# Attention's minus maximum as a row of the zero-padded contraction, in a two-layer sequence net on one core

## What is computed

```python
q = (x @ wq).reshape(Bq, Tq, N_KV, N_REP, HEAD_DIM)
k_lat = (x @ wk_down).reshape(Bq, Tq, N_KV, D_LAT)
v_lat = (x @ wv_down).reshape(Bq, Tq, N_KV, D_LAT)
k = jnp.einsum('bkhl,ld->bkhd', k_lat, wk_up)
scores = jnp.einsum('bqhrd,bkhd->bhrqk', q, k) * scale
scores = jnp.where(causal, scores, jnp.finfo(scores.dtype).min)
probs = jax.nn.softmax(scores, axis=-1)
```

## Time and profile before

| | |
|---|---|
| median of 3 runs | 1990.47 us (1987.96 to 1991.94) |
| the profiled execution, its own time | 1983.65 us |
| its span in the trace | 1981.8 us |
| PE busy | 1660.5 us, 84% |
| DVE busy | 1547.1 us, 78% |
| ACT busy | 1120.8 us, 57% |
| POOL busy | 754.8 us, 38% |

### The profile page before, as it was taken

The page is one execution under the profiler, slowest core; times in us unless marked ns, Lnnn a source line. Parts: engine busy times, 40 slices in busy tenths (PEclk is TensorE's granted clock), DMA queues, the critical chain, the costliest instruction groups (busy, mean ns, idle before and its releaser), DMA issues.

```text
span 1981.8 us, 26962 instructions
## 1 busy us (share of the span) xinstructions
PE 1660.5 (84%) x8352; PEld 768.2 (39%) x8352; DVE 1547.1 (78%) x2173; ACT 1120.8 (57%) x1555; POOL 754.8 (38%) x601
## 2 busy tenths in 40 slices
PE   2434487889997999889997899889998999989988
PEld 0210123344443445344443345344443445434545
DVE  1999899869995899769995899869996999641404
ACT  2445387358744786458744786458744785433232
POOL 0345555324533355324533355324533445310102
PEclk8655699899999999899999999999999999989999
DMA  7999999657955687657955787657955686500000
GB/s 197 228 221 225 227 230 210 150 135 181 230 133 141 158 216 178 156 123 183 231 131 140 159 214 181 156 126 181 232 132 141 165 209 184 130 0 0 6 1 6
DMA packets 107915, 309.48 MB, mean 156 GB/s; under 512 B 15970, under 2 KB 32244, under 8 KB 107764
## 3 DMA queue, kind: packets, MB, share of 16 engines
q1 hardware_dynamic: 93556, 279.32, 59.5%
q10 hardware_dynamic: 14208, 28.32, 4.4%
HBM read 287.67 MB, written 19.92 MB: 155 GB/s over the span
## 4 chain that ended last, share of the span: by engine, by line
PE 36%; DVE 21%; ACT 21%; issue 12%; DMA 5%; ACTq 2%; DVEq 1%; SPq 1%; POOL 0%; POOLq 0%
PE ps_pair L698 8%; PE ps_pair L795 7%; DVE sb_hst L1263 7%; ACT L919 6%; PE ps_pair L854 5%; DMA sb_ring<-spread_dram 5%; PE ps_pair L783 4%; PE ps_pair L874 3%; PE ps_pair L651 3%; ACT sb_ring L950 3%; ACT sb_mix L1099 3%; DVE sb_dd L1241 2%; DVE ps_in L1255 2%; DVE sb_nmax L1404 2%; PE ps_pair L798 2%
## 5 line engine op out<-in xcount | busy, mean ns | idle before, releaser
L1532 POOL TENSOR_TENSOR sb_hc<-sb_hst,sb_crep 128x512 f32<-128x512 f32 x512 | 659.3, 1294 | 990.0 <-DVE sb_hst L1263 617.1
L1263 DVE TENSOR_TENSOR_SCAN sb_hst<-sb_ring,ps_in 128x512 f32<-128x512 f32 x512 | 620.5, 1212 | 21.2 <-ACT sb_ring L950 13.2
L950 ACT ACTIVATE sb_ring<-sb_ring,sb_A 128x512 f32<-128x512 f32 x512 | 345.2, 713 | 227.0 <-DMA sb_ring<-spread_dram 99.5
L1255 DVE TENSOR_TENSOR ps_in<-sb_ring,ps_brow 128x512 f32<-128x512 f32 x512 | 354.3, 692 | 22.1 <-DMA sb_ring<-spread_dram 4.7
L854 PE MATMUL ps_pair<-sb_mix,sb_ew 128*128 128x512 f32 x512 | 251.3, 625 | 19.8 <-ACT sb_h L1065 9.4
L919 ACT ACT_TABLE_LOAD x193 | 247.6, 1283 | 7.3 <-DVE sb_xd L1314 3.2
L633 PE MATMUL ps_y<-sb_hc,sb_const 128*32 128x512 f32 x1024 | 154.2, 677 | 83.0 <-POOL sb_hc L1532 59.4
L795 PE MATMUL ps_pair<-sb_g,sb_h 128*128 128x512 f32 x320 | 170.5, 658 | 23.4 <-DVE sb_dd L1243 11.1
L783 PE MATMUL ps_pair<-sb_h,sb_g 128*128 128x512 f32 (+3 forms) x512 | 165.4, 452 | 6.5 <-DVE sb_nmax L1404 3.2
L854 PEld LDWEIGHTS ps_pair<-sb_mix,sb_ew 128*128 128x128 f32 x512 | 96.0, 198 | 156.7 <-issue 87.1
L874 PEld LDWEIGHTS ps_pair<-sb_ew,sb_eh 128*128 128x128 f32 x1024 | 120.6, 192 | 37.3 <-issue 13.6
(11 more groups left out here) (219 smaller groups left out, 2037.9 us busy)
## 6 DMA issues: line engine op xcount, KB each, us to landing
sb_ring<-spread_dram SPq DMA_DIRECT2D x512, 512.0 KB, 5.6
spread_dram<-sb_dd ACTq DMA_DIRECT2D x32, 512.0 KB, 3.0
sb_brep<-cut_dram ACTq DMA_DIRECT2D x16, 256.0 KB, 3.8
sb_crep<-cut_dram ACTq DMA_DIRECT2D x16, 256.0 KB, 4.2
sb_xtok<-in_L_attn_x_dram SPq DMA_DIRECT2D x8, 256.0 KB, 5.1
sb_ew<-in_L_ffn_w_dram SPq DMA_DIRECT2D x2, 1024.0 KB, 8.5
out_dram<-sb_yy ACTq DMA_DIRECT2D x8, 256.0 KB, 2.3
sb_h<-in_L_ffn_h_w_dram SPq DMA_DIRECT2D x1, 1024.0 KB, 7.0
```

The costliest lines, as they stand in the source:

```text
L950: act.activation(ring[:, n % RING, 0, :], ring[:, n % RING, 0, :], ACT.Exp, scale=A[d][:, g:g + 1]).then_inc(sem["dA"], 1)
L1255: dve.tensor_tensor(ps_in[n % 2][:], ring[:, n % RING, 1, :], ps_brow[:], ALU.mult).then_inc(sem["dbu"], 1)
L1263: dve.tensor_tensor_scan(hst[:, HST_SLOT[n], :], ring[:, n % RING, 0, :], ps_in[n % 2][:], 0.0, ALU.mult, ALU.add).then_inc(sem["scan"], 1)
L1532: pool.tensor_tensor(hc[:, n % 6, :], hst[:, HST_SLOT[n], :], crep[n // NU][:], ALU.mult).then_inc(sem["hc"], 1)
```

## The change

Minus the maximum now enters the score product itself. Each plane of `kz` has rows that are zero; in plane g, row 32 x PARTNER[g] becomes ones (four ACT copies of 1 x 512, semaphore `kone`), and the same row of the query tensor holds minus the maximum in fp32. A partner group's row of q would be needed at the same place by another product, so there are two query tensors, `qT` and `qB`, each with two of the four groups' rows overwritten; ACT copies q twice. `nmax` is a zeroed 128-wide fp32 tensor into which the reductions write at a stride; eight fp32 transposes bring it into both banks of `ps_pair[0]`, and four ACT copies of 1 x 1024 bring the rows to `qT` and `qB`. `split`, `pick`, `mT`'s copy and the pick products are gone. All order tables are new as well.

```diff
-    qT=2, kT=4, kz=1, vlat=1, smax=16, split=2, mT=1, pexp=10, rz=2, yT=2,
+    qT=4, kT=4, kz=1, kone=1, vlat=1, smax=16, mT=4, pexp=10, rz=2, yT=2,
...
+PARTNER = (1, 0, 3, 2)
...
-        elif name[0] == "e" and name[1:].isdigit():
+        elif name == "mT" or name[0] == "e" and name[1:].isdigit():
             mine = PAIRS[0]
...
-        "uxuxuuxuxxguuuuxuuuuuxrxuxurruxuuurxuhuruuuuuxxuururuhuhuruxuuxrruuhuuruuxuuuuhhrguuuuruuuuuuxuuuuuuhuuuruuuuu"
+        "xuruxxuxxuxguuuuxuuuuuxuruxuuruuhruruuxuuhuurruurhuurruururuuuuruhuuuuuhrhguuuuuxuuuuuuruxuhuxrruuuuuuuuuurruu"
...
+        nmax = sb("nmax", [P, 2, REP, P])
+        qB = sb("qB", [P, 2, REP, P])
...
-                        pe.wait_ge(sem["mT"], row("mT", 1))
+                        pe.wait_ge(sem["mT"], row("mT", 4))
+                        pe.wait_ge(sem["kone"], row("kone", 1))
                     for hf, (t, j) in enumerate(units):
-                        pe.matmul(ps_pair[0][:, hf, :], kz[:, 2 * k + hf, j * P:(j + 1) * P],
-                                  qT[:, TILES[hf].index(t), :, :], start=True, stop=False)
-                    for hf, (t, j) in enumerate(units):
-                        ins = pe.matmul(ps_pair[0][:, hf, :], pick[:, 2 * k + hf:2 * k + hf + 1].broadcast_to([P, P]), mT[:, TILES[hf].index(t), :, :],
-                                        start=False, stop=(j < t))
+                        ins = pe.matmul(ps_pair[0][:, hf, :], kz[:, 2 * k + hf, j * P:(j + 1) * P],
+                                        qAB[hf][:, TILES[hf].index(t), :, :], start=True, stop=(j < t))
...
-                pe.wait_ge(sem["split"], row("split", 2))
+                claim("mT")
+                pe.wait_ge(sem["smax"], row("smax", MAXIMA))
                 for tl in range(2):
                     for r in range(REP):
-                        ins = pe.transpose(o[:, tl, r, :], nsplit[:, tl, r, :, :].rearrange("p g c -> p (g c)"), identb[:])
+                        ins = pe.transpose(ps_pair[0][:, tl, r * P:(r + 1) * P], nmax[:, tl, r, :], ident)
...
-                    act.activation(qT[:, :, 2 * half:2 * half + 2, :].rearrange("p t r n -> p r t n"),
-                                   full(f"q{half}")[:].rearrange("p (r t n) -> p r t n", r=2, t=2), ACT.Copy,
-                                   scale=float(D) ** -0.5).then_inc(sem["qT"], 1)
+                    for q in qAB:
+                        act.activation(q[:, :, 2 * half:2 * half + 2, :].rearrange("p t r n -> p r t n"),
+                                       full(f"q{half}")[:].rearrange("p (r t n) -> p r t n", r=2, t=2), ACT.Copy,
+                                       scale=float(D) ** -0.5).then_inc(sem["qT"], 1)
...
-                act.activation(mT, full("mT").bitcast(BF16).rearrange("p (t r n) -> p t r n", t=2, r=REP), ACT.Copy
-                               ).then_inc(sem["mT"], 1)
+                act.wait_ge(sem["full"], row("full", REST_INDEX[f"s{MAXIMA - 1}"] + 1))
+                for g in range(2 * KV):
+                    line = slice(LAT * PARTNER[g], LAT * PARTNER[g] + 1)
+                    ins = act.activation(kz[line, g, :], ones[line, 0:1].broadcast_to([1, T]), ACT.Copy)
+                ins.then_inc(sem["kone"], 1)
+                full("mT")
+                for g in range(2 * KV):
+                    line = slice(LAT * PARTNER[g], LAT * PARTNER[g] + 1)
+                    act.activation(qAB[g % 2][line].rearrange("p t r n -> p t (r n)"), ps_pair[0][line], ACT.Copy
+                                   ).then_inc(sem["mT"], 1)
...
-                    link(dve.tensor_copy(hi, m))
-                    link(dve.tensor_tensor(m, m, hi, ALU.subtract))
-                    link(dve.tensor_copy(mid, m))
-                    dve.tensor_tensor(lo, m, mid, ALU.subtract).then_inc(sem["split"], 1)
...
-                    dve.tensor_reduce(nmax[:, tl, r, :, hf], ps_pair[i % 2][:, :, 0:(t + 1) * P], AX.X, ALU.max,
+                    lines = nmax[:, tl, r, LAT * (1 - hf)::2 * LAT]
+                    dve.tensor_reduce(lines, ps_pair[i % 2][:, :, 0:(t + 1) * P], AX.X, ALU.max,
```

59 lines of the change are left out of this document (20 added, 39 removed).

## The result

The changed kernel takes 2014.94 us (median of 4 runs, 2013.29 to 2018.94) beside 1989.22 of the kernel before (4 runs, 1987.89 to 1991.94): ratio 1.013, 95% interval 1.011 to 1.0151. It is slower by 1.3%, above the range. The profiled execution took 2016.17 us, its span is 2014.3, 32.5 more than before's 1981.8. These 32.5 are: 0.7 ahead of the first attention's last mask, 14.8 in the next five intervals between last masks (before: 1111.6 us, after: 1126.5), 17.0 from there to the end. So 32.5 holds 6.8 us that the median doesn't show, and no run tells in which stretch they lie.

The account below looks back on a forecast made before the run. PE and DVE load bound the 146 us stretch, chains the rest; 3.0 - 6.9 + 7.7 - 5.0 = -1.2 us a pass, times five -6.0, other passes -4.5, together -10.5: 1980.0 us from 1990.47. Range 1957 to 2009.

Parts of the forecast that it names:

- S4: Stretch of 146 us with experts, FFN and score maxima, PE and DVE both the limit: work moved out, -5.0 us.
- e0: First of the ten attention rounds; the forecast was to fail if its products took over 3 us.
- S1: Last masked maximum to first attention round, 4.9 us before: split out, row copies in on the chain, +3.0 us.
- S2: The ten attention rounds, 47.8 us before, a chain of PE and ACT: picks out, other parts swapped, -6.9 us.
- (e): Term of S2: z products just ahead of e6 hold the banks until ACT has emptied them, +3.8 us.
- (f): Term of S2: x0 comes in right behind e6, with products, emptying and steps between, +2.9 us.
- (g): Term of S2: decays of the units and a DMA issue stand ahead of the last exponential, +0.8 us.
- e6: Seventh of the ten attention rounds, with z products ahead of it; forecast some 7.1 us after the round before.
- rival D: A table switch costs twice its load, so the two switches around e6 cost 2.6 us more: 1993 us, chance 0.05.
- S3: Last exponential to the experts' gate products, 24 us before: two dt chains now behind the rounds, +7.7 us.
- The clock's term: Term of S3: PE waits over 4 us ahead of the output product, then runs at the lower clock, +1.0 us.
- Rival A: Loop's end outweighs the rounds: lower clock at two waits of PE, S4 gives back but 3 us; 2008 us, chance 0.30.

Follow-up runs that it names:

- old_order_mT_first: new_row_old_order with transposes moved ahead of x0 on PE, and ones and row copies ahead of x0's DMA on ACT: 1999.44 us, ratio 1.0052.
- new_row_old_order: The changed kernel with the order tables of the kernel before: 2007.71 us, ratio 1.0126.

## Why the prediction was wrong

**The direction.** It forecast -1.2 us a loop pass and measured is +2.44; it forecast -4.5 outside the loop passes and measured is +17.7. Over the five intervals between last masks the sum said -6.0 and +14.8 was measured: a miss of 21 us there and of 22 outside, in the two profiled executions. Two steps carry it: S4, and the passes outside the loop. Of the forecast's own signs of failing one came: e0's products took over 3 us (3.6) in two of the four passes.

**S4, -5.0 forecast, -2.35 measured**: the step that failed in the loop. It counted the work that leaves the stretch (-4.6 on PE) and not what the new tables put in: one sum of the units (1.0 us) in every pass and two to six instructions of the experts' products (0.7 to 2.4 us). PE's busy time fell by 1.9 to 2.2 us in three of the four passes and by 0.8 in the fourth, and S4 followed it. DVE's fell by 5.6 to 6.0, near the forecast 6.7, and bought nothing more: the smaller of the two was to be counted, as the step itself said, but its 4.6 was too large, and the 5.0 it took was larger still.

**S1, +3.0 forecast, +3.75 measured**: the terms were right to 0.15 (2.54 for the ones, 4.1 for the rows); most of the rest is PE's 0.57 of waiting for the reduction ahead of xT. That the transposes now need two banks was in the diff and in no term. In this order it cost nothing; in the old order it is part of the 3.2 us that old_order_mT_first took back.

**S2, -6.9 forecast, -7.4 measured**: the mechanism was right, and the sum in part by luck. Rounds are 3.1 to 3.6 apart, (e) and (f) came at 7.07 and 6.08 (forecast 7.1 and 6.2). The +0.8 of (g) is not there (the last exponential starts 0.12 us behind its mask), and e0 at the lower clock, which no term of S2 had, cost 1.7 in two of four passes; the two cancel. The switches around e6 cost their load of 1.28 and no more. The drain of about 1380 ns a switch that the Trainium skill states beside the load ("ScalarE: Activation LUTs", section What ACT_TABLE_LOAD costs), and with it rival D, is not in this trace.

**S3, +7.7 forecast, +8.4 measured**: the sum was near, its parts were not. ao was 5.7 late and not 4.3 (DVE's 1.71 and 1.66), and that lateness had almost no price: taking it away gave 0.2 us. What cost was the two dt chains as a whole: moving both away gave all 8.3 back to S3. The sum added the delay of ao and the delay of dtp1 as if one followed the other; they end in the same wait, that for the logits, so a gain on one is hidden by the next. That PE itself stands behind the jump when the layernorm's result is there (2.8 us in the pass shown, and 1.97 again) was in no term. How the 8.4 divide between the chains and the jump isn't known. The clock's term of 1.0 measured 1.65.

**Outside the loop, -4.5 forecast, +17.7 measured**: the largest miss, and an estimate "by the loop's terms". It took the second pass to have little of the loop's end, and this is the step's clearest failure: that pass has both dt chains behind its rounds too, its S3 went from 20.29 to 32.43 us, and its S1 to S3 together cost 7.4 us where -1.5 was forecast for the pass. By the cut at last masks this lies in the first interval, and the last loop pass's end in its place outside. Of the +17.0 behind the fifth interval, 8.0 are the last loop pass's end with the final pass's start (S1 +3.8, S2 -6.3, S3 +9.3, S4 +1.2), 3.7 the final pass's (S1 +2.9, S2 -4.1, S3 -1.4, its S4 +6.2: 128.31 against 122.07 us), 5.3 the flush's (S1 +2.9, S2 -0.7, S3 +3.1). The flush has only a row's copies to pay and the picks to gain; why its S2 gains but 0.7 in this execution (2.3 in new_row_old_order) isn't settled (most of it is e1 to e2, 4.89 us against 3.31), nor why the final pass's S4 needs 4.5 to 6.2 us more in every kernel with the new tables.

**Rival A** named the right side and part of the mechanism. Its clock terms were there (1.65 at ao, e0 at the lower level in two of four passes), S4 gave 2.35 and not 3, which is below its point of 2.9; a pass came to +2.44 and not +3.9. Its 2008 lies 7 below the measured 2015 and is near it by luck: it put its five passes 7 us too high and the others, at -2, nearly 20 too low.

**Left open**: where 3 to 6 us come from that the kernels with the row and the old tables lose ahead of the first attention (363.7 to 366.4 us to its last mask against 360.8), and what ends PE's stop behind the jump.

## What to carry to other kernels

Count a stretch's load from the new order, what comes in as well as what goes out. A piece that moves takes its whole trail along: swapping x0 with the transposes and the ones rows was worth 3.2 us in S1, and putting one exponential ahead of a block of DMA issues 3.1 in S2. Before two delays are added, ask whether both end in the same wait. Look at the passes without the loop's jump beside those with it, since the jump can hide a gain. And where a change widens a claim from one bank to two, look at who holds the second.

## What the runs showed of the hardware

A copy of one partition with 1024 elements takes 1.01 us on ACT, as long as one of 128 partitions; two on DVE took 2.46, four memsets of 1 x 512 on DVE 2.37. In the changed kernel the first DVE operation on dt (128 x 512, fp32, L1240) took 0.67 to 0.69 us with POOL idle and 0.67 to 1.71 beside a POOL multiplication, the predicated copy (L1245) 0.72 to 0.74 and 1.66 to 1.68; in the kernel before most of these first operations took 0.66 to 0.72 even beside POOL, so POOL's work alone does not decide it. At the loop's jump PE stood for 3.85 us with nothing that the profile shows ending it, and again for 1.97 between eight products in a row; in the pass that does not jump it stood for 1.11, all of it for DVE.
